# Two-layer transformer megakernel: where the second layer's forty remaining token scatters are issued

## The reference

```python
xn = _layernorm(x, axis=-1)
x = x + _L0_attn_ref(xn, ...) + _L0_ffn_ref(xn, ...)    # 16 heads of 128; 32 experts, 4 per token
xn = _layernorm(x, axis=-1)
x = x + _L1_attn_ref(xn, ...) + _L1_ffn_ref(xn, ...)    # 16 query heads of 16 in 4 groups; 32 experts

# second layer's MoE (rmsnorm of xn first)
scores = jax.nn.softmax(x @ gate_w.T); topk_w, topk_ids = jax.lax.top_k(scores, 4)
buf = zeros((E, C, H)).at[sorted_eid, pos].set(x[tok], mode='drop')   # tokens sorted by expert
eo = (silu(g) * u) @ w2
routed = zeros_like(x).at[tok].add(eo[sorted_eid, pos] * weight)
```

## Time and profile before

| | us |
|---|---|
| median of three runs | 1363.74 (1362.78 to 1365.15) |
| the profiled execution | 1363.39 |
| its span, first to last instruction | 1362.2 |

### The profile page before, as it was taken

The page is one execution under the profiler, slowest core; times in us unless marked ns, Lnnn a source line. Parts: engine busy times, 40 slices in busy tenths (PEclk is TensorE's granted clock), DMA queues, the critical chain, the costliest instruction groups (busy, mean ns, idle before and its releaser), DMA issues. The chain is left out here.

```text
span 1362.2 us, 19842 instructions
## 1 busy us (share of the span) xinstructions
PE 1105.7 (81%) x5536; PEld 830.2 (61%) x5538; DVE 783.0 (57%) x1925; ACT 522.7 (38%) x1419; POOL 511.5 (38%) x487
## 2 busy tenths in 40 slices
PE   6669999999959997788899999778249979999200
PEld 5446667777748986555567778744126758888100
DVE  4967786665025554899986773474115735555233
ACT  2337665555114444355555553311013324444100
POOL 0667775564000000666565560238650000000475
PEclk9879999999969998899999999889559989999655
DMA  9432222221475554222222210245537215555343
GB/s 361 172 97 86 93 94 74 78 71 43 176 183 179 179 180 134 89 78 74 78 71 72 76 53 6 73 174 210 182 130 215 80 59 163 163 163 160 100 126 113
DMA packets 116214, 167.21 MB, mean 123 GB/s; under 512 B 15136, under 2 KB 88736, under 8 KB 113952
## 3 DMA queue, kind: packets, MB, share of 16 engines
q1 hardware_dynamic: 76464, 107.46, 25.0%
q0 software_dynamic: 12288, 33.57, 7.7%
q10 hardware_dynamic: 27360, 24.92, 5.3%
HBM read 103.11 MB, written 62.78 MB: 122 GB/s over the span
## 5 line engine op out<-in xcount | busy, mean ns | idle before, releaser
L1211 PE MATMUL bank<-big_a,probsT 128*128 x760 | 200.2, 359 | 0.0
L856 POOL TENSOR_TENSOR parts<-wq,parts 128x256 fp32r<-128x256 f32 x64 | 49.1, 767 | 380.8 <-ACT parts L1101 380.8
L1110 ACT ACTIVATE probs<-bank,negmax 128x256 f32<-128x256 f32 (+3 forms) x256 | 135.0, 537 | 122.4 <-DVE negmax L1025 114.0
L917 PE MATMUL bank<-kT,qT 128*128 128x256 f32 (+3 forms) x512 | 171.9, 458 | 0.0
L1697 POOL DMA_INDIRECT big_a<-ys_dram,slot_r x64 | 62.1, 970 | 281.1 <-PEq L1680 261.9
L933 PE MATMUL bank<-const,probs 128*128 128x128 f32 x640 | 129.6, 276 | 27.6 <-DVE probs L1037 27.5
L949 PE MATMUL bank<-probsT,big_b 128*128 128x512 f32 (+3 forms) x512 | 149.1, 434 | 0.0
L1211 PEld LDWEIGHTS bank<-big_a,probsT 128*128 128x128 f32 x760 | 131.4, 194 | 20.7 <-issue 1.7
L1289 DVE TENSOR_TENSOR work<-work,bank 128x96 f32<-128x96 f32 (+1 forms) x190 | 51.5, 271 | 159.4 <-ACT work L1256 159.4
L1025 DVE TENSOR_REDUCE negmax<-bank 128x1 f32<-128x256 f32 (+3 forms) x256 | 113.6, 486 | 47.2 <-PE bank L919 46.0
L901 PE MATMUL bank<-parts 128*128 128x512 f32 x256 | 116.9, 492 | 19.8 <-POOL parts L856 15.2
(11 more groups left out here) (208 smaller groups left out, 2011.7 us busy)
## 6 DMA issues: line engine op xcount, KB each, us to landing
probs<-xs_dram SPq DMA_DIRECT2D x190, 128.0 KB
ys_dram<-work ACTq DMA_DIRECT2D x190, 128.0 KB
work<-khT_dram SPq DMA_DIRECT2D x64, 256.0 KB
xs_dram<-big_a SPq DMA_DIRECT2D x12, 1024.0 KB, 20.2
wq<-in_wq SPq DMA_DIRECT2D x64, 128.0 KB
big_a<-in_gu SPq DMA_DIRECT2D x1, 6144.0 KB, 18.5
stack_dram<-parts SPq DMA_DIRECT2D x24, 256.0 KB
xlow<-stack_dram SPq DMA_DIRECT2D x48, 128.0 KB
```

The source lines that it names most:

```text
L917: nc.tensor.matmul(s.ps[bank][:, at:at + w], s.qT[:, par, i * P:(i + 1) * P], s.kT[:, par, 0:w], start=True, stop=False)
L1110: nc.scalar.activation(s.probs[:, par, ROW_AT[i]:ROW_AT[i] + (i + 1) * P], s.ps[bank][:, at:at + (i + 1) * P], ACT.Exp, bias=s.negmax[:, p ...
L1211: mm = nc.tensor.matmul(s.ps[2 + i % 2][:, 0:W], rowsT[:, i % 2, k * P:(k + 1) * P], gu[:, k, bass.ds(e * W, W)], start=k == 0, stop=k == ...
```

## The change

POOL's list in `attention_block1` is cut into sixteen parts of two or three scatters, and ahead of each part POOL waits until DVE has built the shift of one more head. The scatters are the same 40, in the same order, and the final waits for their landing stay. Nothing on any other engine changes.

```diff
         @block.gpsimd
         def _(pool):
-            for t in range(EARLY_TILES, TILES):
-                scatter_tile(nc, s, d, 1, t, moved)
+            late = [(t, k) for t in range(EARLY_TILES, TILES) for k in range(TOPK)]
+            for u in range(NU):
+                pool.wait_ge(shift_ready, u + 1)
+                for t, k in late[len(late) * u // NU:len(late) * (u + 1) // NU]:
+                    scatter_tile(nc, s, d, 1, t, moved, (k,))
             for k in range(TOPK):
                 pool.wait_ge(moved[k], 16 * (TILES - EARLY_TILES))
```

## The result

| | kernel before | changed kernel |
|---|---|---|
| median of the comparison | 1364.16 us (4 runs, 1362.78 to 1365.15) | 1327.23 us (4 runs, 1326.87 to 1328.92) |
| span of the profiled execution | 1362.2 us | 1325.7 us |
| mean granted clock | 0.911 | 0.921 |
| block: from ACT's table load to the next block's | 148.22 us (959.15 to 1107.37) | 112.48 us (959.18 to 1071.66) |

The account below looks back on a forecast made before the run. PE's signals, held back during the long row of scatters, were taken to bound the block's early heads. Savings of 34.4 us there and 1.0 at PE's start sum to 35.4: 1363.74 to 1328.3 us, range 1324 to 1338.

Parts of the forecast that it names:

- the hole: Second attention block, 978 to 1016 us: PE busy only 9.7 of 38 us while POOL works all the time.
- PE from its start to head 3's products: Second attention block, first matmul to head 3's products: forecast 21.5 us instead of 55.87, a saving of 34.4 us.
- The clock term: Block's early heads: two heads' work counted as one at full clock, 4.77 us, and one mostly at lower clock, 7.98.
- The first piece: PE's first gapless stretch in the block, from 969.08 to 977.85, at clock 0.50: expected to stay at 8.77 us.
- PE's start: Block's start, PE waiting for `sums` behind the first loads: without scatters there, 0 to 1.8 us won, 1.0 taken.
- The load of the DMA engines: Eight heads: scatters share the engines with loads, 4.9 us per head against 4.77; cost taken as 0, bound 5 us.
- The lead of three heads: In the block, a stack is loaded nearly three heads, 13 us, before it is needed, hiding any DMA deficit.
- The cover at the block's end: Last three scatters, released by DVE's last shift, done by 1096; next block begins at 1107.37, leaving 11 us.
- the hold: Second attention block: PE's signals delivered late, one every 3 to 8 us, blamed on the long run of scatters.
- The hold has another cause: Rival: something in the block's first two heads delays the signals, PE waits as before, 1363.7 us; chance 0.05.
- It needs scatters and a loaded DMA system: Rival: late signals need both together; in eight heads with large weight loads 22 us return, 1350; chance 0.07.
- Each scatter holds for its own time: Rival: every scatter beside a working head delays PE's signals 1.24 us, 50 us instead of 36, 1378; chance 0.04.

Follow-up runs that it names:

- experiment 9: Changed kernel with the load of the row sums issued ahead of the first heads' stack loads, chip 2: 1320.13 us, ratio 0.9943 to the kernel before.
- experiments 4: Kernel before, forty scatters in a row from the start, weight loads of heads 0 to 11 moved to heads 4 to 15, chip 11: 1327.97 us.
- 5: Kernel before, unchanged, run again with a trace on chip 4: 1362.68 us, ratio 0.9997.
- experiment 8: Kernel before, forty scatters in a row from the start, weight loads of heads 0 to 11 moved to heads 4 to 15, chip 2: 1325.53 us.
- 10: Kernel before, forty scatters in a row from the start, weight loads of heads 0 to 11 moved to heads 4 to 15, chip 13: 1328.75 us.
- 1: Kernel before with the block's forty scatters left out, and with them part of the output, chip 11: 1326.91 us beside 1325.91.
- experiments 2: Kernel before with the forty scatters in four rows of ten, released at heads 0, 4, 8 and 12, chip 11: 1328.31 us.
- 3: Kernel before with all forty scatters in one row, released only by the shift of head 4, chip 11: 1326.48 us beside 1325.91.
- 6: The changed kernel again, against the kernel before on chip 4: 1326.75 us, ratio 0.9737.
- 7: Kernel before with all forty scatters in one row, released only by the shift of head 4, chip 2: 1328.34 us beside 1327.77.
- 11: Kernel before with all forty scatters in one row, released only by the shift of head 4, chip 11: 1327.24 us beside 1325.96.
- 12: The changed kernel again, against the kernel before on chip 0: 1327.43 us beside 1363.29, ratio 0.9738.

## Why the prediction was right, and where its ground was too thin

**What bounds the kernel: right.** PE's signals came late in the hole, and once they came in time the block was PE's own work, 75.32 of 76 us.

**PE from its start to head 3's products: right, 20.93 us against 21.5.** The clock term was one head at each pace, 4.77 and 7.98 us. It rested on one rise of the clock, seen in the trace before, and experiment 9, where the rise came a head sooner, shows that this could have come out otherwise. PE took 7.62 us from head 1's products to head 2's (976.74 to 984.36) and 4.77 us to head 3's. The first piece was 8.54 us, not 8.77. By these terms the saving is 34.94 us, 0.5 over the forecast.

**PE's start: right, 0.88 us against 1.0** (969.08 to 968.20). The other traces agree: PE waits 18.5 to 18.9 us for `sums` in the five with the scatters in front (the kernel before, experiments 4, 5, 8, 10), and 17.6 to 18.1 us in the eight with none in front (the changed kernel, 1, 2, 3, 6, 7, 11, 12).

**The load of the DMA engines: right.** From 978 to 1016 us the queues read as follows in the changed kernel (against the earlier trace rows):

```profile
q1 hardware_dynamic: 3960, 8.50, 74.9%
q0 software_dynamic: 826, 2.25, 15.1%
```

Together they have work for 90% of the time, so they nearly bind; but the only wait of PE in these heads is the one at the start. The lead of three heads held.

**The cover at the block's end: held.** The last scatter is issued at 1053.90 and the next block starts at 1071.66, 17.8 us later.

**The sum** was 35.4; the block is 35.7 us shorter, the spans differ by 36.5 and the medians by 36.9. The 0.8 us between block and span lie behind the block (254.8 us to the end before, 254.0 after), and are not traced further.

**The cause: half right.** The prediction took the row of forty scatters as the whole cause. On chips 4 and 0 and in the comparison, dealing them out removed the hold three times (0.9735, 0.9737, 0.9738). But the row stood unchanged on chips 11, 2 and 13, and cost nothing. It is a needed part at most, together with something of the place. And the change does two things at once: it breaks the row up, and it starts it 12.7 us later (972.54 in place of 959.86), behind the block's first loads; no run with the hold tells these apart. The sizes of the forecast were worked out and held; that there was a hold to remove was luck of the place, since beside the kernel before on chips 11, 2 or 13 the same forecast would have been some 35 us off. None of the rivals was this one. "The hold has another cause" fails as written, since the change did remove the hold. "It needs scatters and a loaded DMA system" is false as a full account, since the kernel before has both on chips 11, 2 and 13. "Each scatter holds for its own time" fails by the changed kernel's trace.

The rule that had been weighed against the change, in the Trainium skill's page "SBUF — State Buffer", section "Who interferes with whom", is that PE and ACT never wait on anyone; the section is about the ports through which engines reach SBUF. Read as widely as the prediction tried it, it gave 1363.7, and the three comparisons contradict that reading: ACT's exponential came 13 us late while scatters ran, and came in time once they were dealt out. What ACT waited for was a signal and not an access to SBUF, so these runs say nothing against the rule on its own ground.

**What stays open.** (1) What differs between the places. The chip is the plain candidate: chip 11 gave no hold in both of its groups, chip 4 gave it in 23 of 23 runs of the kernel before. But the groups with the hold had only the kernel before and the changed one in them, and the groups without it had other kernels too; since each chip but one was seen in one group, the runs can't tell these two apart. (2) How long or how dense a row must be there, whether its start ahead of the block's first loads matters, and whether loaded DMA engines take part: experiments 2, 3 and 4 were made for these and met chips without the hold. (3) What exactly is held. The traces show PE's signals late and their events missing, not the path. Whether the hold exists when nothing is recorded is open too.

## What to carry to other kernels

When several engines wait for one engine's signals long after its work is done, and the profile names no sensible releaser, look for the engine that works without a pause in that stretch and try spreading its work: here that brought 2.6% where the hold was, at no measured cost. Time the kernel before beside each experiment, on the same chip: eight runs made to take the cause apart could not do so because the hold was not there, and only the kernel before's own time told so. Order the loads at a stage's start by who needs them first: a 64 KB load behind twelve of 128 KB cost PE 4.65 us, and in the one trace that shows it about 2.7 more through a clock that rose later.

## What the runs showed of the hardware that had not been expected

- One kernel on one core has two times 37 us apart, 1325.9 to 1329.0 and 1360.4 to 1366.3 us, and each holds for all runs of a group. The changed kernel takes 1326.75, 1327.23 and 1327.43 us in the three groups where the kernel before takes over 1360 us; it was not timed elsewhere.
- Where the hold exists it repeats: the block took 148.22 and 148.23 us in two groups of runs, with ACT's late starts within 0.9 us of each other and DVE's within 2.2 us.
- Forty indirect scatters in a row, one every 1.30 us, beside DMA engines busy 81% of the time, left PE busy 38.0 of 38 us on chip 2 (experiment 8).
- The five traces from places with the hold lack releasers all through the program (13 to 21 waits of ACT each), the other nine lack none on ACT; and the end of the program, behind the issue of the last store, is 1.2 to 2.0 us longer in the five.
- The granted clock went from its lower to its higher level (1.2 to 2.4 GHz) 14.5 us after PE's first matmul in the changed kernel (it is 0.64 from 982 to 983 us and 1.00 from then on), and 13.6 to 14.7 us after it in all the other traces without late signals but one. In experiment 9 it was 8.8 us (0.81 from 974 to 975 us, then 1.00). All had worked without a gap since their start; ahead of it PE had rested 17.6 to 18.7 us in the others and 12.96 us in experiment 9. What made the difference is not shown; here the earlier start was worth more than itself.
